# Grouped-query attention: scores on four row tiles without masked key copies, issued group by group, and turned copies on VectorE

## The reference

```python
h  = _rmsnorm(hidden_states, ln1_w)
kv = _rmsnorm(kv_states, ln1_w)
q = (h @ Wq) ...    # 16 query heads of 64
k = (kv @ Wk) ...   # 4 key heads of 64
v = (kv @ Wv) ...   # 4 value heads of 64
q = _apply_rope(q, cos_q, sin_q); k = _apply_rope(k, cos_k, sin_k)
k = jnp.repeat(k, 4, axis=1);     v = jnp.repeat(v, 4, axis=1)
scores = jnp.einsum('bhqd,bhkd->bhqk', q, k) / math.sqrt(HD) + attention_mask
probs  = jax.nn.softmax(scores, axis=-1)
attn   = jnp.einsum('bhqk,bhkd->bhqd', probs, v) @ Wo
hidden = residual + attn
```

## Time and profile before

| | |
|---|---|
| three runs | 1665.19, 1667.31, 1672.28 us |
| median | 1667.31 us |
| the profiled execution | 1668.44 us, its span 1666.6 us |
| TensorE matmuls busy | 1390.1 us, 83% of the span |
| VectorE busy | 696.3 us, 42% |
| ScalarE busy | 623.5 us, 37% |
| GpSimd busy | 377.4 us, 23% |
| mean granted clock of TensorE | 0.907 |

### The profile page before, as it was taken

The page is one execution under the profiler, slowest core; times in us unless marked ns, Lnnn a source line. Parts: engine busy times, 40 slices in busy tenths (PEclk is TensorE's granted clock), DMA queues, the critical chain, the costliest instruction groups (busy, mean ns, idle before and its releaser), DMA issues. The chain is left out here.

```text
span 1666.6 us, 28785 instructions
## 1 busy us (share of the span) xinstructions
PE 1390.1 (83%) x11090; PEld 962.7 (58%) x11090; DVE 696.3 (42%) x1394; ACT 623.5 (37%) x1549; POOL 377.4 (23%) x473
## 2 busy tenths in 40 slices
PE   4999999655299999974666797998998899787997
PEld 2666666444299999962444345545554455554665
DVE  2677676524121000005554561262253336134666
ACT  2444444110144554431222272164237127214442
POOL 4224540022400000013331341052033124006200
PEclk9999999855599999996777799999999999998999
DMA  9900000003289999961000000000000000000000
GB/s 347 413 33 2 2 2 2 2 0 126 86 285 331 321 328 329 333 217 39 26 26 0 1 1 1 0 0 0 0 0 0 0 0 0 0 0 1 14 15 27
DMA packets 83144, 137.89 MB, mean 83 GB/s; under 512 B 5336, under 2 KB 63712, under 8 KB 83040
## 3 DMA queue, kind: packets, MB, share of 16 engines
q1 hardware_dynamic: 78672, 127.02, 21.8%
q0 software_dynamic: 3072, 8.39, 1.5%
q10 hardware_dynamic: 1296, 1.02, 0.2%
HBM read 107.32 MB, written 29.10 MB: 82 GB/s over the span
## 5 line engine op out<-in xcount | busy, mean ns | idle before, releaser
L369 PE MATMUL bank<-reg 128*128 128x512 f32 x416 | 192.9, 626 | 12.6 <-PEq L229 9.1
L1260 ACT ACTIVATE w_ca<-scores,fc1b 128x128 f32<-128x128 f32 x312 | 114.1, 368 | 138.5 <-PE scores L1216 118.2
L821 ACT ACTIVATE reg<-scores 128x1024 f32<-128x1024 f32 x96 | 93.1, 1021 | 161.5 <-PE scores L625 161.5
L369 PEld LDWEIGHTS bank<-reg 128*128 128x128 f32 x416 | 81.1, 201 | 120.7 <-issue 98.3
L1216 PEld LDWEIGHTS scores<-reg 128*128 128x128 f32 x1248 | 147.7, 194 | 4.6 <-issue 2.7
L1216 PE MATMUL scores<-reg 128*128 128x128 f32 x1248 | 148.1, 278 | 2.1 <-issue 1.1
L882 DVE TENSOR_REDUCE reg<-scores 128x8 f32<-128x1024 f32 x96 | 113.0, 1220 | 71.4 <-PE scores L615 71.4
L1226 PE MATMUL bank<-reg,w_ca 128*128 128x256 f32 x624 | 141.1, 379 | 0.3 <-DVE small L1273 0.3
L1226 PEld LDWEIGHTS bank<-reg,w_ca 128*128 128x128 f32 x624 | 115.6, 190 | 14.5 <-DVE small L1273 0.3
L449 POOL TENSOR_TENSOR reg<-reg,rden 128x512 f32<-128x512 f32 x80 | 83.1, 1041 | 157.7 <-DVE rden L1760 88.9
L1582 PE MATMUL scores<-reg 128*128 128x512 f32 x256 | 117.5, 594 | 0.0
(11 more groups left out here) (236 smaller groups left out, 2251.5 us busy)
## 6 DMA issues: line engine op xcount, KB each, us to landing
reg<-in_fc SPq DMA_DIRECT2D x78, 1024.0 KB, 7.2
expert_rows<-reg SPq DMA_DIRECT2D x36, 480.0 KB, 14.6
reg<-expert_rows SPq DMA_DIRECT2D x39, 128.0 KB, 5.6
expert_rows<-reg SPq DMA_DIRECT2D x39, 128.0 KB, 6.5
xres<-in_x SPq DMA_DIRECT2D x1, 2048.0 KB, 11.6
ctxr<-in_ctx SPq DMA_DIRECT2D x1, 2048.0 KB, 8.6
w_l<-in_w_l SPq DMA_DIRECT2D x2, 1024.0 KB, 12.2
out<-xres SPq DMA_DIRECT2D x8, 256.0 KB, 2.6
```

Source lines behind the costliest of these rows:

```text
L369: ins = nc.tensor.matmul(bank[:, 0:n], w[:, c, w0:w0 + P], src[:, c, :], start=(c == 0), stop=(c == C - 1))
L821: ins = nc.scalar.activation(PT2[:, t % 2, 2 * half:2 * half + 2, :, :, :].rearrange("p r s c q -> p (r s c q)"), scores4[:, 2 * half:2 * ...
L1260: nc.scalar.activation(h1[:, j % 2, f, :], S[n % 4][:, 0:P], ACT.Gelu, bias=fc1b[:, bass.ds(e * FC + f, 1)]).then_inc(M["fc1_free"], 1)
```

## The change

The masked copies `kM2`, the eight ScalarE instructions a pass that make them and the wait for them go. `scores(j)` now fills all four banks for batch j: bank `S[i]` belongs to key head i and holds its four query heads side by side; each matmul contracts the 32 partitions of head i, on row tile i, with 128 columns, and the two halves h are added up in the bank. One signal `scored` stands for the four banks. Before group 0 it waits, query pair by query pair, for `roped`. The later groups are issued ahead of turn m = 0, 4 and 8, behind the wait for all mask additions of the group before. The turned copies go from ScalarE to VectorE, six tiles behind the mask additions, and the reciprocals are taken four tiles behind, not two. The products read the tiles of one key head from neighbouring places. `kr` moves in the working memory.

```diff
@@ -187,8 +187,7 @@
         qr = view(12288, [GB, 2, NT])
-        kr = view(0, [2, NT])
-        kM2 = view(16384, [NKV, 2, NT])
+        kr = view(16384, [2, NT])
@@ -1576,11 +1575,17 @@
-                    def scores(j, a):
-
-                        for h in range(2):
-                            ins = nc.tensor.matmul(S[a][:, :], qr[:, a, h, j * P:(j + 1) * P],
-                                                   kM2[:, :, h, j * P:(j + 1) * P], start=(h == 0), stop=(h == 1))
+                    def scores(j):
+
+                        at_j = slice(j * P, (j + 1) * P)
+                        for a in range(A4):
+                            if j == 0:
+                                pe.wait_ge(M["roped"], 2 * (a + 2))
+                            for h in range(2):
+                                for i in range(NKV):
+                                    r = slice(i * HALF, (i + 1) * HALF)
+                                    ins = nc.tensor.matmul(S[i][:, a * P:(a + 1) * P], qr[r, a, h, at_j], kr[r, h, at_j],
+                                                           start=(h == 0), stop=(h == 1))
                         ins.then_inc(M["scored"], 1)
@@ -1591,22 +1596,17 @@
-                                                       PT[:, j % 2, i::NKV, :],
+                                                       PT[:, j % 2, A4 * i:A4 * (i + 1), :],
...
-                    pe.wait_ge(M["keys_ok"], 2)
-                    for a in range(A4):
-                        pe.wait_ge(M["roped"], 2 * (a + 2))
-                        scores(0, a)
-                    for n in range(4 * GB + TURN_LAG):
-                        if n + 4 < 4 * GB:
-                            pe.wait_ge(M["masked"], n + 1)
-                            scores(n // 4 + 1, n % 4)
-                        m = n - TURN_LAG
-                        if m >= 0:
-                            pe_turn(pe, m)
+                    scores(0)
+                    for m in range(4 * GB):
+                        if m % 4 == 0 and m + 4 < 4 * GB:
+                            pe.wait_ge(M["masked"], m + 4)
+                            scores(m // 4 + 1)
+                        pe_turn(pe, m)
@@ -1671,27 +1671,12 @@
-                    for h in range(2):
-                        act.wait_ge(M["roped"], h + 1)
-                        for i in range(NKV):
-                            ins = nc.scalar.activation(kM2[:, i, h, :], kr[:, h, :], ACT.Copy, scale=of_key_head[:, i:i + 1])
-                        ins.then_inc(M["keys_ok"], 1)
                     values()
-                    N, LAG = 4 * GB, COPY_LAG
-                    for n in range(N + LAG):
-                        if n < N:
-                            act_exp(act, n, bank_of(n)[0])
-                        if n >= LAG:
-                            m = n - LAG
-                            act.wait_ge(M["turned"], m + 1)
-                            if m >= 8:
-                                await_full(act, J, f"pv{m // 4 - 2}_1")
-                            nc.scalar.activation(turned_tile(m), T[m % 2][:, :].rearrange("p (s q) -> p s q", q=P),
-                                                 ACT.Copy).then_inc(M["pt_ok"], 1)
-
-                        j = (n - 7 - LAG) // 4
-                        if 0 <= j < GB - 1 and n == 4 * j + 7 + LAG:
-                            out_copies(j)
+                    for n in range(4 * GB):
+                        act_exp(act, n, bank_of(n)[0])
+                        if n % 4 == 3 and n >= 11:
+                            out_copies(n // 4 - 2)
+                    out_copies(GB - 2)
                     out_copies(GB - 1)
@@ -1741,11 +1726,11 @@
-                    N = 4 * GB
-                    for n in range(N + 2):
+                    N, DIV_LAG, TURN_AFTER = 4 * GB, 4, 6
+                    for n in range(N + TURN_AFTER):
                         if n < N:
                             j = n // 4
-                            dve.wait_ge(M["scored"], n + 1)
+                            dve.wait_ge(M["scored"], j + 1)
@@ -1755,9 +1740,17 @@
-                        if n >= 2:
-                            dve.wait_ge(M["probs"], n - 1)
-                            nc.vector.reciprocal(cols_of(rden, n - 2), cols_of(psum, n - 2)).then_inc(M["divided"], 1)
+                        if DIV_LAG <= n < N + DIV_LAG:
+                            m = n - DIV_LAG
+                            dve.wait_ge(M["probs"], m + 1)
+                            nc.vector.reciprocal(cols_of(rden, m), cols_of(psum, m)).then_inc(M["divided"], 1)
+                        if n >= TURN_AFTER:
+                            m = n - TURN_AFTER
+                            dve.wait_ge(M["turned"], m + 1)
+                            if m >= 8:
+                                await_full(dve, J, f"pv{m // 4 - 2}_1")
+                            nc.vector.tensor_copy(turned_tile(m), T[m % 2][:, :].rearrange("p (s q) -> p s q", q=P))\
+                                .then_inc(M["pt_ok"], 1)
```

## The result

The changed kernel takes 1703.12 us (median of four runs, 1698.86 to 1704.96) where the kernel before takes 1668.60 in the runs beside it: a ratio of 1.0203, 95% interval 1.0173 to 1.0233, some 34.5 us slower. The forecast was 1712 us in a range of 1676 to 1735. The span of the profiled execution grew from 1666.6 to 1697.1 us.

The account below looks back on a forecast made before the run. TensorE was taken as the bound, its matmul rows filling 43.4 of a pass's 47.98 us. At full clock +2.9 us a pass, the clock +8, so +10.9, 44 in four passes: 1668.4 + 44 - 1 = 1712 us, range 1676 to 1735.

Parts of the forecast that it names:

- start: First mask addition of a pass: starts 0.4 us later, since it waits for the whole group of scores.
- VectorE's 15 steps: First to last mask addition: 4 steps of 1.33, 2 of 1.43, 9 of 2.04 us, 26.6 us against 32.1 before.
- idle times: VectorE waiting for scores of groups 1, 2 and 3: 9.4 us a pass at full clock, 6.8 more by the clock.
- tail: Last mask addition to output projection: 12.3 us at full clock, 1.4 less than 13.74; the fallen clock adds 1.2.
- A burst of scores on row tiles: One group's scores on TensorE: 64 instructions take 2.2 us instead of 6.9; adding two halves in a bank costs nothing.
- the rival without overlap: Row tiles don't run beside each other: 6.9 us a burst, 19 us a pass more, 1755 us; chance 0.03.
- VectorE's step: Mask addition, maximum, reciprocal and turned copy on VectorE: 2.04 us with both reciprocal and copy, the copy about 0.60.
- The chain: Late reciprocals, scaling and turns delay the next scores: VectorE idles 1.9, 3.6 and 3.9 us ahead of groups 1 to 3.
- The faster rival: VectorE never idles between groups, copies and reciprocals fill the gap: -6.5 us a pass, 1641 us; chance 0.03.
- The clock: TensorE, idle between bursts, falls toward half clock in the attention passes: +8 us a pass, bounds 0 and +19.
- The clock holds: Rival: TensorE's clock stays full in the attention passes, only the +12 us of four passes remains, 1679 us; chance 0.12.
- Copies of keys: Eight masked key copies on ScalarE, hidden since they ended 9.5 us ahead of the first scores: removal worth nothing.

Follow-up runs that it names:

- kept busy: Changed kernel plus matmuls of no use on TensorE in the idle stretches of its attention part, written to a free bank: 1681.46 us, ratio 1.0070.
- the kernel with the shorter chain: Changed kernel with reciprocals two tiles behind, copies five, scores of groups 2 and 3 behind turns 2 and 6, and added matmuls: 1653.43 us, ratio 0.9911.
- the short schedule: Kernel with the shorter chain, every second turned copy moved to ScalarE: 1646.75 us with added matmuls (moved to other places), 1665.69 us without.
- the fastest: Kernel with the shorter chain, added matmuls kept but partly moved, every second turned copy on ScalarE instead of VectorE: 1646.75 us, ratio 0.9874.

## Why the prediction was right, step by step

The passes by the terms of the sum. The kernel before has 2.12 us from the first scores to the first mask addition, 32.12 from there to the last and 13.74 of tail; the first pass after has 2.33, 40.99 and 14.79.

| Term, us a pass | Predicted | Measured, passes 1 and 4 | At full clock (kept busy) |
|---|---|---|---|
| start | +0.4 | +0.2, +0.2 | +0.2 |
| VectorE's 15 steps | 26.6 | 26.2, 26.1 | 26.2 |
| idle times | 9.4, and 6.8 by the clock | 14.8, 13.9 | 8.9 |
| tail | 12.3, and 1.2 by the clock | 14.8, 14.1 | 12.5 |
| the pass against before | +10.9 | +10.1, +8.7 | +2.1 |

- **A burst of scores on row tiles: right.** 2.2 us were forecast from half a burst of the first layer; the next work stands 2.00 us behind its start in the kernel kept busy. Adding up two halves in a bank costs nothing that the trace shows, so the rival without overlap (1755 us) is out.
- **VectorE's step: right.** 2.04 us forecast, 1.99 measured; the copy's price, taken from another layer, held in this one.
- **The chain: right in each of its three places.** 1.9, 3.6 and 3.9 us were forecast at full clock, 1.59, 3.44 and 3.91 measured in the kernel kept busy. The faster rival, which had VectorE idle for less than 6.5 us, is out: with the reciprocal where it is, there is one copy of 0.6 us in a chain of over 4. Of the 0.3 us by which the first one is shorter, 0.2 are the burst (2.0 us, not 2.2).
- **The clock: right in its kind, a little too dear.** 8 us were taken, 7.0 measured (28 us in four passes, not 32). The 4.97 us ahead of scores(1) and the half-rate burst behind them came as said: the burst is 3.80 us, not 4.4. It ran at half rate to its end at 970.03; each four of its instructions stand 0.21 us behind the four before, where they stand 0.11 us behind in the kernel kept busy. The clock came back behind it. By the idle times at full clock (1.59, 3.44, 3.91) and the tail (12.5), the fallen clock cost 1.7 us ahead of group 1 (taken: 2.2), 1.4 us ahead of group 2 in the first pass and 1.8 in the last (taken: 2.6), 2.7 and 1.4 ahead of group 3 (taken: 2.0), and 2.3 and 1.5 in the tail (taken: 1.2). The term most overpriced is group 2, for which I had turn 3 and scores(2) cold from end to end; in the first pass the clock comes back within the burst (its last instructions are at the full rate). Group 3 and the tail were priced too low. In the first pass these errors cancel, 8.2 us measured for 8.0 taken, which is luck; in the last pass it is 6.5. "The clock holds" (1679 us) is what the kernel kept busy shows, 1681 us, so that rival's price was about right as well, and its condition was not met. That the two agree to 2 us is luck in part: its passes cost 8.6 us against before, not 12, and the rest came from the stretches between them.
- **Copies of keys: worth nothing, as said.**
- **The tail** was forecast 1.4 us shorter at full clock and is 1.2 us shorter (12.5). The kernel with the copies alone on VectorE shows a gain of 2.6 us (11.1). The other 1.4 us point to the distances: the kernel with the shorter chain, with reciprocals two tiles behind and copies five, has row tiles and a tail of 10.7 us at full clock.
- **The total** came out 9 us under the forecast: 7 to 8 by the passes (36.5 us for 44). The rest is within what one kernel does from run to run (the kernel before: 1665.19 to 1672.28). The forecast's own last sum, 1668.4 + 44 - 1, gives 1711, not 1712; nothing hangs on that.

The rule of the Trainium skill that was set against the change (TensorEngine Tiling (Array Packing), Performance Considerations, that the emptying of banks doesn't get faster) was half of the story. VectorE's steps are on the path, but they alone would have made the pass shorter (26.2 us for 32.1). What cost time was the wait between groups: with four row tiles writing four banks, a group needs all four to be empty, and here it also stood behind turns that wait for a late reciprocal. The second of these was the larger. With whole groups still, but scores behind turns 2 and 6 and shorter distances, 3.4 us of the 8.9 us of idle time are left.

The Trainium skill has a rule for the other half (TensorE: Matmul & The Clock Gate, the section on why this matters for your kernels): no long pause between bursts of matmuls, or the clock drops. The trace agrees, with 2.07 against 3.80 us for the same 64 instructions, the second time behind 4.97 us of pause. Short pauses are no safeguard, though: in the kernel with the shorter chain the clock of the first pass fell to 0.50 between 993 and 994 us, and TensorE had had no pause above 1.4 us in that pass.

What wasn't tried is the obvious other repair, to issue row-tiled scores tile by tile as before: then TensorE would write one part of a bank while VectorE reads another part of the same bank, and the semaphores as they are would not order the two.

## What to carry to other kernels

Work taken from the engine that is the bound counts only as far as the order of issue lets the next engine use it. Before an operation is made to fill several banks at once, follow the chain from the release of the last bank back to itself, through every engine, and put the issue ahead of whatever in the queue waits for the slowest link.

A TensorE that has become fast enough to wait may run at half its clock. Price each burst at both levels. Where pauses can't be closed, matmuls of no use into a free bank can pay: 28 us in the four passes here, of which 22 are left in the whole time, and 19 of the whole time in the short schedule, for no change of the real work.

Of a change with several parts, the parts are best timed alone. The copies on VectorE were 0.6% faster by themselves, in a change that was 2% slower.

## What the runs showed of the hardware that I had not expected

The kernel with the scores computed twice lost 5.3 to 5.9 us between each two passes, in code that was not touched. TensorE's first projection of the next pass is late, once with the scores twice and once in the changed kernel:

```profile
1103.63 8.92 PE L368 MATMUL bank<-reg 128*128 128x512 f32 x16 [5.72 <-issue]
```

```profile
1087.11 5.42 PE L368 MATMUL bank<-reg 128*128 128x512 f32 x12 [2.39 <-PEq L228]
```

Of this, 3.3 us are the longer pause. The rest goes with the clock, 0.93 in the stretch between the passes for 0.96, and need not follow from the pause: the kernel kept busy has 0.93 there and up to 93.4 us with a pause of 2.39 us. The queue that carries instructions, on the two pages (with the scores twice, and changed), has 29 packets more:

```profile
q8 instruction: 104, 1.70, 0.4%
```

```profile
q8 instruction: 75, 1.23, 0.3%
```

A packet of this queue is 16 KB (1.70 MB by 104), and one such transfer, 16 GB/s for one microsecond, lies in each of the three long pauses; the short ones of the changed kernel have none. In the first of either:

```profile
1100.00:1101.00 1.00, 0.00 (x0) 0.00 (x0) 0.00 (x0) 0.83 (x1) 0.00 (x0) 0.72 0.07 16
1086.00:1087.00 1.00, 0.00 (x0) 0.00 (x0) 0.00 (x0) 0.02 (x1) 0.00 (x0) 1.00 0.00 0
```

A turn of the loop has 882 matmuls and as many weight loads on TensorE there (610 in the pass, 272 between), against 627 in the changed kernel. It looks as if its loop body no longer stays where the instructions are kept and is fetched again each time. The packets, their place in the pause and the pause are measured; that the one causes the other is argued: no run changed the length of the loop without changing its work. The kernel with the added matmuls (30625 instructions in all, not 32333) still has the pause of 2.39 us.

Also unexpected was how regular a schedule without clock changes can be: in three kernels at 1.00 throughout their passes (kept busy, copies alone on VectorE, the fastest), the four passes agree to 0.03 us (49.91 to 49.94, four times 45.21, four times 42.80). Where the clock falls they differ by up to 2.4 us in one execution (56.42 and 58.83 in the kernel with the key copies kept), though the scores computed twice had them within 0.07.
